# A state-space stage in a four-block kernel: D times u computed by ScalarE into the sum's buffer, and all eight products of a group added by GpSimd

## The reference

```
def step(h, inp):
    d_t, u_t, b_t, c_t = inp
    dA = jnp.exp(d_t[..., None] * A)
    h = dA * h + (d_t * u_t)[..., None] * b_t[:, None, :]
    y_t = jnp.einsum('bdn,bn->bd', h, c_t)
    return (h, y_t)
...
y = jnp.swapaxes(ys, 0, 1) + u * D_param
y = y * jax.nn.silu(z)
return jnp.einsum('bld,ed->ble', y, out_proj_w)
```

## Time and profile before

| | |
|---|---|
| median of 3 runs | 483.39 us (480.75, 483.39, 483.78) |
| profiled execution | 475.68 us, its span 473.9 us |
| busy, share of the span | TensorE 74%, VectorE 77%, ScalarE 64%, GpSimd 50% |
| mean granted TensorE clock | 0.888 of full speed |
| costliest group of VectorE | scan, line 1899, 32 x 1785 ns = 57.1 us |
| costliest groups of GpSimd | line 480 (attention) 54.4 us; line 511 (adds) 27 x 1887 ns = 51.0 us |

### The profile page before, as it was taken

How to read it: one execution, slowest core, us unless ns; L and a number is a source line. 1 busy time by engine, 2 the same in 40 slices (tenths; PEclk the granted TensorE clock), 3 DMA queues, 4 the chain that set the end, 5 groups by cost and what they waited for, 6 DMA issues and landing times. The chain is left out here.

```text
span 473.9 us, 10025 instructions
## 1 busy us (share of the span) xinstructions
PE 348.7 (74%) x3480; PEld 228.1 (48%) x3480; DVE 366.4 (77%) x681; ACT 301.8 (64%) x585; POOL 235.2 (50%) x217
## 2 busy tenths in 40 slices
PE   4159888895889785986876746567775719988885
PEld 3046666664755432242232212122573519877774
DVE  4799999998896397889987999996777675644443
ACT  4328788888784999478859944528985343333432
POOL 4527868776573416956982997666281220000000
PEclk9568999999899998588988876878999758999999
DMA  6110000000314150022000000000000000111111
GB/s 147 5 18 4 3 0 0 0 1 0 87 32 96 24 116 2 0 67 50 1 1 0 0 1 0 0 0 1 2 0 1 3 0 11 20 19 22 22 19 24
DMA packets 23876, 9.49 MB, mean 20 GB/s; under 512 B 20520, under 2 KB 22312, under 8 KB 23848
## 3 DMA queue, kind: packets, MB, share of 16 engines
q1 hardware_dynamic: 23720, 9.13, 9.4%
q0 software_dynamic: 128, 0.01, 0.2%
HBM read 2.00 MB, written 1.61 MB: 8 GB/s over the span
## 5 line engine op out<-in xcount | busy, mean ns | idle before, releaser
L480 POOL TENSOR_TENSOR Pr<-Pr,rc 128x392 f32<-128x392 f32 x64 | 54.4, 883 | 31.6 <-DVE rc L1831 31.5
L511 POOL TENSOR_TENSOR YA<-YA,hC 128x784 f32<-128x784 f32 x27 | 51.0, 1887 | 31.8 <-DVE hC L1915 30.9
L1353 PE MATMUL pair<-BCf,sel 96*128 96x392 bf16 x128 | 38.3, 392 | 33.8 <-DVE Hs L1899 29.9
L1899 DVE TENSOR_TENSOR_SCAN Hs<-dA,pair 128x784 f32<-128x784 f32 x32 | 57.1, 1785 | 1.0
L1197 PE MATMUL pair<-ident,Pr 128*128 128x128 f32 x256 | 40.7, 289 | 13.2 <-ACT PT L715 8.4
L1353 PEld LDWEIGHTS pair<-BCf,sel 96*128 96x128 bf16 x128 | 10.1, 104 | 72.7 <-issue 69.6
L1197 PEld LDWEIGHTS pair<-ident,Pr 128*128 128x128 f32 x256 | 28.5, 144 | 25.9 <-ACT PT L715 15.1
L1892 DVE TENSOR_TENSOR pair<-DU,pair 128x784 f32<-128x784 f32 x32 | 31.1, 973 | 10.5 <-PE pair L1353 10.2
L715 ACT ACTIVATE PT<-pair 128x392 f32<-128x392 f32 x64 | 31.3, 496 | 6.1 <-PE pair L1197 5.9
L724 ACT ACTIVATE Pr<-Ts 128x392 f32<-128x392 f32 x64 | 32.5, 536 | 3.1 <-DVE Ts L1815 3.0
L1809 DVE TENSOR_REDUCE mx<-pair 128x8 f32<-128x392 f32 x64 | 32.6, 550 | 1.1 <-PE pair L1154 1.0
(11 more groups left out here) (264 smaller groups left out, 925.5 us busy)
## 6 DMA issues: line engine op xcount, KB each, us to landing
SX<-XP SPq DMA_DIRECT2D x48, 112.2 KB
XT<-in_x SPq DMA_DIRECT2D x4, 392.0 KB, 4.7
out<-Os SPq DMA_DIRECT2D x28, 56.0 KB, 1.8
NB<-in_L_conv_x_proj_w SPq DMA_DIRECT2D x4, 3.0 KB
DW<-in_L_conv_dw SPq DMA_DIRECT2D x4, 1.1 KB
vec<-in_L_conv_b_qkv POOLq DMA_DIRECT2D x3, 0.5 KB, 5.6
W<-in_L_conv_w_qkv SPq DMA_DIRECT2D x1, 48.0 KB
BL<-in_L_conv_bi SPq DMA_DIRECT2D x3, 0.5 KB
```

What stands on the lines that cost most here:

```text
L480: eng.tensor_tensor(pg, pg, bcast(rc[:, g, :], 2, WT), ALU.mult).then_inc(pn_r, 1)
L511: eng.tensor_tensor(y, y, hC[:, n % NHC, :], ALU.add).then_inc(g_ya, 1)
L1353: ins = eng.matmul(SPREAD[s][:, columns(h)], sel[:, n, :], upper(BCf[:, c % 2, s, columns(h)]), start=True, stop=True)
L1899: eng.tensor_tensor_scan(Hs[:, n % 2, :], dA[:, n % NA, :], SPREAD[0], 0.0, ALU.mult, ALU.add).then_inc(v_s, 1)
```

## The change

ScalarE now begins each group c by writing D times u into `YA[:, c % 2]`, for all four groups (`skip_term(c)` in `act_ssm`; from group 2 on it waits until the outputs of group c - 2 have read that buffer). All eight products go into the ring hC, and GpSimd adds all eight to YA: product 0 waits for ScalarE's D times u, the others for the add before. The GpSimd `skip_term` of group 3 is gone, and `outputs` of groups 0 to 2 is one VectorE product, YA x ZS. The counts of the ring and of `g_ya` go from seven to eight a group.

```
--- before.py
+++ after.py
...
             def add(c, n):
 
                 eng.wait_ge(v_c, DS * c + n + 1)
-                if n > 1:
-                    eng.wait_ge(g_ya, (DS - 1) * c + n - 1)
+                if n:
+                    eng.wait_ge(g_ya, DS * c + n)
+                else:
+                    eng.wait_ge(a_ud, c + 1)
                 y = YA[:, c % 2, :]
                 eng.tensor_tensor(y, y, hC[:, n % NHC, :], ALU.add).then_inc(g_ya, 1)
...
-            def skip_term():
-
-                eng.wait_ge(a_ud, 1)
-                eng.wait_ge(v_c, DS * (J - 1) + 1)
-                y = YA[:, (J - 1) % 2, :]
-                eng.tensor_tensor(y, y, S1[:, 0, 0:T], ALU.add).then_inc(g_ud, 1)
...
             def pool_ssm(i):
                 if i == 0:
+                    add(0, 0)
                     add(0, 1)
...
                 elif i == 1:
                     remainder(2)
                     split(2, 0, "xB")
+                    add(1, 0)
                     add(1, 1)
...
                     plus_log(3)
+                    add(2, 0)
                     add(2, 1)
...
                     later_weights()
-                    skip_term()
-                    eng.wait_ge(g_ud, 1)
+                    add(3, 0)
                     add(3, 1)
...
+            def skip_term(c):
+                if c >= 2:
+                    eng.wait_ge(v_y2, c - 1)
+                eng.activation(YA[:, c % 2, :], US[:, c, :], ACT.Identity, scale=vec[:, V_D:V_D + 1]).then_inc(a_ud, 1)
+
             def act_ssm(i):
                 if i == 0:
+                    skip_term(0)
                     silu_u(1, 0)
...
                 elif i == 1:
+                    skip_term(1)
                     sp_abs(2, 0)
...
                 elif i == 2:
+                    skip_term(2)
                     sp_abs(3, 0)
...
                 else:
-                    eng.activation(S1[:, 0, 0:T], US[:, J - 1, :], ACT.Identity, scale=vec[:, V_D:V_D + 1]).then_inc(a_ud, 1)
+                    skip_term(3)
                     decays(3, 4, 5)
...
             def ring_free(c, n):
 
-                before = (DS - 1) * c + n - NHC if n > NHC else (DS - 1) * c + min(n - NHC, 0)
-                if before > 0:
-                    eng.wait_ge(g_ya, before)
+                if DS * c + n >= NHC:
+                    eng.wait_ge(g_ya, DS * c + n - NHC + 1)
 
             def times_c(c, n):
                 eng.wait_ge(p_["C"], DS * c + n + 1)
                 eng.wait_ge(v_s, DS * c + n + 1)
-                if n == 0:
-                    dst = YA[:, c % 2, :]
-                else:
-                    dst = hC[:, n % NHC, :]
-                    ring_free(c, n)
-                eng.tensor_tensor(dst, Hs[:, n % 2, :], SPREAD[1], ALU.mult).then_inc(v_c, 1)
+                ring_free(c, n)
+                eng.tensor_tensor(hC[:, n % NHC, :], Hs[:, n % 2, :], SPREAD[1], ALU.mult).then_inc(v_c, 1)
...
             def outputs(m):
-                eng.wait_ge(g_ya, (DS - 1) * (m + 1))
+                eng.wait_ge(g_ya, DS * (m + 1))
                 if m:
                     eng.wait_ge(p_["out"], m)
-                eng.scalar_tensor_tensor(yz[:, :], US[:, m, :], vec[:, V_D:V_D + 1], YA[:, m % 2, :], ALU.mult, ALU.add).then_inc(v_y1, 1)
-                eng.wait_ge(v_y1, m + 1)
                 eng.wait_ge(c_["z"], m + 1)
-                eng.tensor_tensor(yz[:, :], yz[:, :], ZS[:, m, :], ALU.mult).then_inc(v_y2, 1)
+                eng.tensor_tensor(yz[:, :], YA[:, m % 2, :], ZS[:, m, :], ALU.mult).then_inc(v_y2, 1)
...
-            eng.wait_ge(g_ya, (DS - 1) * c + DS - 2)
+            eng.wait_ge(g_ya, DS * c + DS - 1)
...
-                eng.wait_ge(v_y1, J + h)
+                eng.wait_ge(v_y1, h + 1)
...
```

More of the change, by code:

```diff
@@ L220, in build @@
         v_b, v_s, v_c, v_cc, v_dl, v_du, v_y1, v_y2, v_nt, v_n0, v_c7 = sems("v_b v_s v_c v_cc v_dl v_du v_y1 v_y2 v_nt v_n0 v_c7")
-        g_ya, g_ml, g_cw, g_mid, g_low, g_nt0, g_ud, g_w, s1z = sems("g_ya g_ml g_cw g_mid g_low g_nt0 g_ud g_w s1z")
+        g_ya, g_ml, g_cw, g_mid, g_low, g_nt0, g_w, s1z = sems("g_ya g_ml g_cw g_mid g_low g_nt0 g_w s1z")
         t_pr, t_g, t_z, t_t, t_o, t_sg, t_gd, t_za, t_q, t_sd, t_ye, t_yg = sems("t_pr t_g t_z t_t t_o t_sg t_gd t_za t_q t_sd t_ye t_yg")
```

## The result

The changed kernel took 482.95 us in the median of 22 runs (478.89 to 484.81), the kernel before 479.30 us in 22 runs beside it. The ratio is 1.0083, with a 95% interval from 1.0059 to 1.0107: slower by some 0.8%, a little less than the 1% that the prediction set as its bound, where it had said 0.3%. The ratios leave out runs that lie over 1.5% above the fastest of their kernel, six of the 22 of the kernel before in this set and none of the changed kernel's. Over all 22 runs of each the medians differ by 3.65 us and the means by 2.85.

What follows compares the result with a forecast made beforehand. VectorE bounds two stretches, with TensorE at half clock from 187 to 204; 0.87 + 0.87 + 0.87 - 0.15 - 1.2 = +1.3 us, from 483.39 to 484.7 us, range 480.5 to 488.0.

Steps and rivals of the forecast that it cites:

- the band of 0 to +2.5: Whole kernel: the forecast outcome, a change between 0 and +2.5 us, given a chance of 0.46.
- Group 0, +0.87: New ACTIVATE ahead of silu_u(1,0) delays the copy of xC, TensorE's convolution and VectorE: +0.87 us.
- Group 1, ScalarE, +0.87, and saving 0: New ACTIVATE before sp_abs(2,0) delays VectorE at 228 by 0.87 us; the 1.03 us saved in outputs(0) become waiting.
- Group 1, GpSimd, -0.15: Extra add moves delta(2) later; the add that delta_u(2) meets ends some 0.15 us sooner: -0.15 us.
- the good end (-1.0): Group 1, GpSimd term: -1.0 us if delta_u(2) meets no GpSimd add; the other end is +1.85.
- Group 2, +0.87, saving 0: New ACTIVATE delays line 809's ReLU, x_c(3) and VectorE's spread: +0.87 us; the 1.03 us saved in outputs(1) lengthen the wait.
- Group 3, -1.2: outputs(2) becomes one product: gain about 1.9 us running free or 0.5 meeting line 558; middle taken, -1.2 us.
- The end of 0.5: Group 3: if outputs(2)'s product meets line 558's broadcast product, it waits until about 293.5; gain 0.5 us.
- The cap of 1.9 us: Group 3: a free product's gain is capped at about 1.9 us by the spread behind wout(1) and out(2).
- Rival (2): Longer wait before group 1's convolution drops TensorE's clock, four states cost +3.6: in all +4.9 us, 488.3; chance 0.10.
- Two of my signs: The part behind the state stage lasts as before; forecast wrong if a stretch shows another granted clock than before.
- rival 1: ScalarE's work is hidden and all of VectorE's saving counts: -4.6 us, 478.8; chance 0.18 with its partial form.

Runs made afterwards that it cites:

- the third: The changed kernel a third time, no edit, against the kernel before: ratio 1.0078 (1.0043 to 1.0114).
- the second: The changed kernel a second time, no edit, against the kernel before: ratio 0.9995 (0.9964 to 1.0025).
- the first two of before: First and second profiles of the kernel before, no edit: state stage 148.85 and 152.30 us.
- the ACTIVATE alone: The kernel before plus the three ACTIVATEs of groups 0 to 2, written into a tile nobody reads: ratio 1.0022 (0.9977 to 1.0067).
- VectorE's part alone: The kernel before with outputs of groups 0 to 2 as one product, D times u left out of their result: ratio 0.9917 (0.9869 to 0.9966).
- the second pair: Second profiles of the kernel before and the changed kernel, no further edit: stage 152.30 and 152.49 us.
- The first pair: First profiles of the kernel before and the changed kernel, no further edit: stage 148.85 and 150.09 us.
- the add of group 3 first: The changed kernel with all three ACTIVATEs moved, and GpSimd's add(3,0) in front of later_weights: ratio 0.9888 (0.9835 to 0.9942) against the kernel before.
- the second profile of before: The kernel before profiled again, no edit: state stage 152.30 us, the part behind it 155.88 us.

## Why the prediction was right or wrong

The sign and the class were right (slower, by less than 1%), and the measured times lie in the range. The size was not: +1.3 us forecast, +4.0 us by the first ratio (0.0083 x 479.3), about 3.7 by the third, none by the second. Two of the three are outside the band of 0 to +2.5 that had the chance of 0.46. That 484.7 came within 2 us of 482.95 is luck: it was built on a median of three runs, 483.39, which lies 4.1 us above the median of 22, and this error and the too small step nearly cancel.

- **Group 0, +0.87.** Right, and the best shown: +0.83 to +0.85 at scan (0,4) in three profiles against the first two of before; there with the ACTIVATE alone, and gone when it moved.
- **Group 1, ScalarE, +0.87, and saving 0.** Right where the clock is full: +0.83, and gone when the ACTIVATE moved. The saving was taken up by the spreads, as the kernel with VectorE's part alone and the one with this ACTIVATE moved show.
- **Group 1, GpSimd, -0.15.** delta_u(2) took 0.97, 2.28 and 1.97 us in the three profiles; before 1.98, 2.11 and 1.99. So anywhere between the good end (-1.0) and +0.3. I missed norm(0): 2.52 us in the first profile of the changed kernel, where it met the last adds, and 1.15 before. It lay in VectorE's wait for the spread of state 2 and cost nothing there.
- **Group 2, +0.87, saving 0.** Right: +0.89 at full clock, and with low stretches in both +0.80 in the second pair and +0.96 with the ACTIVATEs alone. The first pair shows nothing in this step (12.36 us in both). TensorE's wait grew there as in the others (3.37 for 2.53), but the step began later: scan (2,0) started 2.79 us behind ScalarE's decays in front of it and not 1.86, with norm(0) at 2.52 us.
- **Group 3, -1.2.** This is the term that was mis-sized. I took the middle of an outcome that has no middle. The product took 0.97 us once (-2.6 in its step) and 3.04 and 3.17 us in the other two (-0.5 and -0.4), because line 553 had started 0.2 to 0.3 us earlier:

```profile
298.38 3.04 DVE L1931 TENSOR_TENSOR yz<-YA,ZS 128x784 f32<-128x784 f32 x1
```

```profile
298.06 2.53 POOL L553 TENSOR_TENSOR BD<-W,bd 128x1408 f32<-128x1408 f32 x1
```

The rule that the prediction quoted, from the Trainium skill (SBUF — State Buffer, Who interferes with whom), gave these two ends and nothing between. The end of 0.5 turned out the likelier: of the seven profiles with the changed kernel's GpSimd queue in group 3, six have it. With it the sum would have been +2.0 us. The cap of 1.9 us on the good end was too low: the step lost 2.6 us in the first profile, and again with the add of group 3 first. In the first profile line 553 was just over when VectorE asked (291.45 + 2.53, against 294.14), and VectorE had lost 1.87 us to the kernel before in the step ahead, at a lower clock; over (2,2) to (3,2) the three pairs differ by -0.7, -0.7 and -0.6 us.
- **The rest.** Rival (2) described something real (low stretches in group 1) but put it down to one cause. Between scans (1,1) and (1,4) they come in executions of the kernel before as well, in one of three profiles, and in two of three of the changed kernel; where they fell in both, its step was no longer than before. With three profiles each, a difference in how often they fall is not shown. About 2.2 us (0.84 + 0.83 + 0.89 - 0.4) is what the steps show of the change itself. The remaining 1 to 2 us of the two slower ratios I can't assign; the means of all runs differ by 2.85, 0.16 and 2.53 us in the three sets, which lies around the 2.2.
- **Two of my signs were wrong as tests.** The part behind the stage took from 152.96 to 155.88 us in profiles of one kernel. And I had called myself wrong if a stretch showed another granted clock than before: several did (0.90 for 1.00 from 228), but so did they in the kernel before from one profile to the next.
- **The face value (rival 1)** failed because of where the ACTIVATEs stand. With them moved, the same change is faster than the kernel before by 0.5 to 1.0%, of which the steps account for a part only.

## What to carry to other kernels

Moving an operation to an engine that is 64% busy says nothing until you know who waits for that engine at that place in its queue: here three instructions of 0.87 us, put in front of work that TensorE was waiting for, cost their full length, and put a few lines on, into waits for TensorE, the same three cost nothing. Where two engines exclude each other, the one that asks second waits for what is left of the other's instruction: here 0.97 us became anything up to 3.2. If both ask within 0.3 us of each other, that is close to all or nothing; forecast one of the two ends and not the middle, and arrange that the engine on the path asks first. And before a fraction of a per cent is read from one pair of profiles, profile the same kernel again: here one program's stage moved by 5 us, and its granted clock with it.

## What was not expected of the hardware

- The low stretches of TensorE's clock fall at different places in different executions of one program. That of 187 came in all 14 profiles, within 2 us of the end of a wait of 3.4 to 3.7 us. Elsewhere a fall came or didn't come behind waits of equal length: in group 1 (220 to 224 and 227 to 231 in the second profile of before), and in group 2, where behind the changed kernel's wait of 3.37 us x_c(3) ran at once at the low clock in two profiles and at full speed in the third (1.53 us and not 2.90). The Trainium skill (TensorE: Matmul & The Clock Gate, What's actually happening) says that how many matmuls run at the half clock when a kernel starts varies from run to run of one kernel. The profiles here show such a variation in the middle of a kernel.
- A tensor_scalar of VectorE with one SBUF input (padded) waited for GpSimd too: 1.91 us for 0.68. The Trainium skill (SBUF — State Buffer, Who interferes with whom) names tensor_scalar among the instructions that can; I had applied it to instructions with two SBUF inputs only.
